# Both halves of the values product in one stretch, instead of one in each half-step behind its job

## What is computed

```python
xn = layernorm(x)
# attention, which norms xn once more with its own gain and bias
q, k, v = (z @ W + b).reshape(B, S, 16, 8)          # z: the second norm
p = (pe @ Wp).reshape(S, 16, 8)
content = einsum('bihd,bjhd->bhij', q + u_bias, k)
pos = relative_shift(einsum('bihd,jhd->bhij', q + v_bias, p))
attn = softmax((content + pos) * 8 ** -0.5)
head = einsum('bhij,bjhd->bihd', attn, v)           # the values product
x = x + head @ Wo + bo + mlp(xn)                    # mlp: 256 -> 512 -> 512 -> 128, relu
```

## Time and profile before

| | |
|---|---|
| median of three runs | 1458.08 us |
| lowest and highest | 1455.66, 1462.42 us |
| profiled execution, first to last instruction | 1453.5 us |
| granted TensorE clock, mean | 0.997 |
| busy TensorE, VectorE, ScalarE, GpSimd | 1441.7, 1357.5, 1226.6, 754.8 us |
| DMA | 550.41 MB, mean 379 GB/s |

### The profile page before, as it was taken

One profiled execution on the slowest core, in us unless ns is written; L12 is line 12 of the kernel. 1 busy time (PEld: TensorE's weight loads), 2 busy tenths in 40 slices (PEclk: granted clock), 3 DMA queues, 4 the chain that ended last, 5 costly groups with the idle time before them and its releaser, 6 DMA issues.

```text
span 1453.5 us, 41653 instructions
## 1 busy us (share of the span) xinstructions
PE 1441.7 (99%) x16170; PEld 977.4 (67%) x16170; DVE 1357.5 (93%) x3489; ACT 1226.6 (84%) x1365; POOL 754.8 (52%) x753
## 2 busy tenths in 40 slices
PE   8999999999999999999999999999999999999999
PEld 4566666666676666766666676666766666666666
DVE  6899999999999999999999999999999999999996
ACT  5688888888888898888888888888888888888874
POOL 5575555555655565454655555566554645543410
PEclk9999999999999999999999999999999999999999
DMA  5999999999999999999999999999999999999992
GB/s 197 385 399 394 383 404 386 389 391 379 409 377 399 394 386 397 377 399 383 397 398 373 408 376 397 397 377 407 382 391 392 384 398 380 394 380 389 396 397 108
DMA packets 80867, 550.41 MB, mean 379 GB/s; under 512 B 9376, under 2 KB 10528, under 8 KB 15136
## 3 DMA queue, kind: packets, MB, share of 16 engines
q1 hardware_dynamic: 43376, 278.61, 49.5%
q10 hardware_dynamic: 37296, 269.15, 47.9%
HBM read 274.57 MB, written 273.15 MB: 377 GB/s over the span
## 4 chain that ended last, share of the span: by engine, by line
PE 95%; DMA 2%; ACT 1%; DVE 1%; issue 0%; SPq 0%; ACTq 0%
PE ps_pt L853 35%; PE ps_av L867 19%; PE ps_pos L829 14%; PE ps_job L756 12%; PE ps_job L720 4%; PE ps_job L710 3%; PE ps_job L735 2%; PE ps_con L841 1%; PE ps_job L731 1%; DMA shift<-pos_sb 1%; ACT pt_sb L514 1%; PE ps_job L743 1%; PE ps_job L726 1%; DMA sc_sb<-shift 1%; DMA heads<-in_pe_t 0%
## 5 line engine op out<-in xcount | busy, mean ns | idle before, releaser
L673 DVE CUSTOM_DVE_ANT_0 sc_sb<-ps_con,sc_sb 128x512 f32<-128x512 f32 x1024 | 661.9, 682 | 65.0 <-PE ps_con L841 61.5
L500 ACT COPY pos_sb<-ps_pos 128x1024 f32<-128x1024 f32 x510 | 518.0, 1016 | 180.4 <-PE ps_pos L829 169.4
L681 DVE TENSOR_SCALAR sc_sb<-sc_sb,nmax 128x512 f32<-128x512 f32 x1024 | 629.2, 646 | 0.1
L853 PE MATMUL ps_pt<-c_sb,sc_sb 128*128 128x128 f32 x4048 | 553.5, 280 | 2.5 <-ACT pt_sb L514 1.5
L514 ACT ACTIVATE pt_sb<-ps_pt 128x1024 f32<-128x1024 f32 x506 | 519.1, 1026 | 20.1 <-PE ps_pt L853 18.8
L853 PEld LDWEIGHTS ps_pt<-c_sb,sc_sb 128*128 128x128 f32 x4048 | 433.9, 141 | 127.1 <-issue 93.2
L867 PE MATMUL ps_av<-pt_sb,v_sb 128*9 128x128 f32 x8192 | 319.9, 274 | 0.1
L867 PEld LDWEIGHTS ps_av<-pt_sb,v_sb 128*9 128x9 f32 x8192 | 172.8, 90 | 184.4 <-issue 182.2
L841 PE MATMUL ps_con<-k_stack,q_stack 26*128 26x512 f32 x1024 | 267.5, 496 | 1.8 <-DVE nmax L673 1.5
L396 POOL CAST h<-act_sb 128x512 fp32r<-128x512 f32 x128 | 78.1, 610 | 360.7 <-ACT act_sb L473 357.4
L829 PE MATMUL ps_pos<-p_stack,q_stack 26*128 26x512 f32 x1024 | 259.6, 496 | 1.2 <-ACT pos_sb L500 0.9
(11 more groups left out here) (116 smaller groups left out, 1015.8 us busy)
## 6 DMA issues: line engine op xcount, KB each, us to landing
shift<-pos_sb SPq DMA_DIRECT2D x256, 1026.0 KB, 9.3
sc_sb<-shift ACTq DMA_DIRECT2D x256, 1024.0 KB, 9.8
x_sb<-in_x SPq DMA_DIRECT2D x16, 256.0 KB, 11.8
out<-x_sb SPq DMA_DIRECT2D x15, 256.0 KB, 10.5
c_sb<-in_consts ACTq DMA_DIRECT2D x1, 288.0 KB, 6.8
sc_sb<-in_wp SPq DMA_DIRECT2D x1, 256.0 KB, 5.8
sc_sb<-in_stack_w ACTq DMA_DIRECT2D x1, 256.0 KB, 5.5
heads<-in_pe_t SPq DMA_DIRECT2D x1, 256.0 KB, 6.9
```

Source lines behind the costliest of these rows:

```text
L500: act.copy(to, ps_pos[:, :, :]).then_inc(s_pe, 1)
L673: dve.tensor_tensor_reduce(sc_sb[:, m % N_SC, t, :], ps_con[:, k, :], sc_sb[:, m % N_SC, t, :], -SCALE, 3.4e38, ALU.add, ALU.min, nmax[:, ...
L681: dve.tensor_scalar(sc_sb[:, m % N_SC, t, :], sc_sb[:, m % N_SC, t, :], nmax[:, m % N_SC, t:t + 1], None, ALU.subtract).then_inc(s_sub, 1)
L853: last = pe.transpose(pt_banks(k)[:, j % 2, t * P:(t + 1) * P], sc_sb[:, u % N_SC, t, j * P:(j + 1) * P], id_sb)
```

## The change

Up to block 500 the values are no longer issued one block to a half, behind the job. In a half whose transposes are those of a unit's first half (k even; these halves are odd), TensorE issues both value blocks of the unit before, k - 2 and k - 1, between the scores and the transposes. In a half with k odd it issues none. `SINGLE` is 2 * 256 - 11 = 501: from the transposes of block 501 on, which stand in half 518, the values stand where they did, and the last units are unchanged. The waits inside `values` and `turn` are the same. `valued` is also what places VectorE's copy of `ps_av`, in the half after the one that does the fourth unit's last block; that half stays the same.

```diff
+        SINGLE = 2 * UNITS - 11
...
         def valued(h):
 
-            return [k - 1 for k in turned(h) if k] + [2 * UNITS - 1] * (h == TURN_AT[-1] + 1)
+            pairs = [v for k in turned(h) if 0 < k < SINGLE and k % 2 == 0 for v in (k - 2, k - 1)]
+            return pairs + [k - 1 for k in turned(h) if k >= SINGLE] + [2 * UNITS - 1] * (h == TURN_AT[-1] + 1)
...
                 turns, products = turned(half), valued(half)
+                if products and products[0] < SINGLE - 1:
+                    for k in products:
+                        values(*divmod(k, 2))
+                    products = []
                 for k in turns[:1]:
                     turn(*divmod(k, 2))
                 for j in parts(half):
```

## The result

Four runs of the changed kernel gave 1483.14 to 1486.87 us, a median of 1484.56, against 1456.87 for the kernel before on the same chip. The ratio is 1.0185, 95% interval 1.0159 to 1.0212. Lines of the changed kernel stand three further down: the transposes are line 856, the values 870, the exponential 517, reduce and subtraction 676 and 684.

A forecast was written before the change was run, and what follows sets the result against it. TensorE, busy 99%, sets the pace, VectorE and ScalarE close behind. Per batch -1.76 + 2.43 + 0.4 + 0.3 = about +1.35, over 15.5 batches +21: span 1474.5, plus 4.6 around it, 1479 us; range 1461 to 1492.

The forecast's parts named there:

- Handover saved: Two value blocks back to back on TensorE save one handover per unit: 0.11 each, 1.76 per batch.
- (c): Scores to values in the long half costs 0.33, not 0.44: 3.5 saved per batch against 3.1 of waits, 1452; chance 0.09.
- (d): TensorE handovers at the mean of three kinds: 0.17 saved per unit, 2.7 per batch against 3.1, 1465; chance 0.06.
- Wait for the exponential: Short half's transposes, without values before them, wait for the long half's exponential: 2.43 per batch.
- the 2.27 from load to load: Least distance the exponential allows between transposes of adjacent halves with no job between: 2.27 us.
- its sign of being wrong: Forecast is wrong if, among other signs, the short half's transposes start under 2.2 after the long half's.
- ScalarE's chain: Exponential, evacuation, score copy and next exponential delay the long half's second value block: about 0.4 per batch.
- VectorE's rhythm: Uneven halves make VectorE's reduces late for the second contents product: 1.15 per batch, net 0.3 after today's waits.
- The walk: Stepping VectorE through a batch with today's intervals: contents late 0.45 by half 3, 0.42 at half 17; 1.15 per batch.
- Ends: Halves with no job at both ends wait 0.8 instead of 0.25: 2 more, less 2 where waits coincide.
- Rival (a): The exponential's wait swallows ScalarE's and VectorE's knock-on waits: 0.67 x 15.5 = 10, plus 2 at the ends, 1470; chance 0.20.
- Rival (b): VectorE stays late after short halves, reduces on the path in a third of units: another 0.7 per batch, 1490; chance 0.10.

The follow-up runs named there:

- e7: Changed kernel with the exponential of each unit's first half split by bank and GpSimd's split instructions cut to 64 columns; 1436.04 us (0.9854).
- e1: Kernel before with GpSimd's two split instructions cut to 64 of 512 columns from the third batch on; 1448.37 us (0.9957).
- e2: Changed kernel with GpSimd's two split instructions cut to 64 of 512 columns from the third batch on; 1457.24 us (1.0017).
- e9: Kernel before with values paired only in two units of 16, long halves 21 and 31 of 32; ratio 1.0015.
- e3: Kernel before with its single value block per half moved between scores and transposes, one half later, and the ps_av copy behind VectorE's reduces; 1482.34 us (1.0196).

## Why the prediction was right, and which term was off

The forecast was 1479 us, the result 1484.56, inside the range; the side and the two mechanisms hold. By the prediction's own steps:

- **Handover saved**, -1.76 per batch: -1.78 in e7 against e1, and 0.11 in halves 22 and 23 by themselves. Scores to values 0.44, job to scores as job to values. Right, and with it rivals (c) and (d) fall.
- **Wait for the exponential**, +2.43: 1.87 in e2. The places are right (halves 4, 8, 12, 20, 24, 30 with 0.3 each; 10, 16, 28 with 0.05), the size 0.56 too large. The step that was off is the 2.27 from load to load, read from one pair of halves; there the bracket of the second row names VectorE's subtraction as what came last, and not the exponential. In the kernel after it is 2.20 (743.55 to 745.75), since 0.05 and not 0.12 passes behind the exponential. That is the very edge of what the prediction had called its sign of being wrong. The code says that these are waits for `s_exp`, and the split exponential took them away. The total that the profile puts down to the exponential rose from 10 to 83.4 us, not to some 45.
- **ScalarE's chain**, +0.4: 0.1 to 0.2, a term too small to matter.
- **VectorE's rhythm**, net +0.3: about 1.5, the difference between 1.85 and 0.31. This is the term that was mis-sized, by a factor of five. The walk took "the intervals of today" for VectorE, and these don't stay: a subtraction's time depends on whether GpSimd is at work, and the change moves the jobs that GpSimd follows. I had counted only how late VectorE would start, not that its work would grow by 43 us. The walk's gross figure was 1.15, with 0.45 in half 3 and 0.42 in half 17; in the long halves contents are late by 1.82, with 0.19 in half 3 and 0.67 in half 17. The netting against today's 0.8 was too much as well: late contents are only 0.37 of that in the trace before, and the cut on GpSimd took 0.48 off a batch.
- **Ends**, +2 less 2: 28.7 of the span's 31.5 are 15.5 batches of 1.85, so 2.8 are left.

The trace before already held what was missed. The 3.43 that the prediction takes from the earlier trace rows isn't the distance of two scores, as it says, but that of VectorE's first reduces in two halves, and inside it lies a subtraction that GpSimd had made long:

```profile
709.10 1.28 DVE L681 TENSOR_SCALAR sc_sb<-sc_sb,nmax 128x512 f32<-128x512 f32 x1
```
```profile
708.83 1.27 POOL L387 TENSOR_TENSOR k_stack<-act_sb,k_stack 128x512 fp32r<-128x512 f32 x1
```

Part of the hit is luck. Exponential and ScalarE were 0.8 too high, VectorE 1.2 too low, so the batch came to +1.85 and not +1.35. And the 4.6 us that were added for what lies around the span were 1.8 to 1.9 in every run measured since: the forecast missed the time by 5.6 us, but the spans, 1481.3 to 1485.0, lie 7 to 10.5 above its 1474.5.

Rival (a), that the knock-on waits are swallowed, is close to what the runs with the cut show, 9 us, and wrong for the full kernel. Rival (b), with +2.05 per batch, 1490 us and late contents in a third of the units, is as near to the result as the forecast, and nearer in its batch and its reason: contents are late in the long halves of 6 of the 16 units. It had the right engine, but VectorE isn't late for good; its late starts come back in the same halves of every batch, and what makes it late is its own longer subtractions.

TensorE's busy time did not fall or stay, as the prediction had it, but rose by 12 us. The same 1024 contents products show 295.6 us busy instead of 267.5, at 0.494 and 0.496 us for one; a second product that comes late overlaps the first less. Busy time isn't work.

What stays open is how much of VectorE's 1.5 is overlap with GpSimd in the strict sense and how much is a fuller VectorE meeting an unevenly spaced TensorE. The cut takes both away at once, as it also frees 0.15 us per subtraction. A run with GpSimd's work whole and VectorE's cut otherwise wasn't made.

## What to carry to other kernels

A block that is moved on the bounding engine is also a cover that is moved: list for each wait what stands between its two ends before and after, and its price follows from start-to-start distances. Where two engines slow each other down, durations read from the old trace are no constants; a change that only shifts jobs in time can add work on an engine it doesn't touch. And in a schedule with just 0.8 us of waits in 87.6, look for the price of a local saving some halves further on: the pair in halves 20 and 21 saved 0.13 where it stood and cost 0.37 in half 24.

## What the runs showed that I had not expected

A subtraction of 128x512 in SBUF takes 0.47 to 0.49 us alone, and beside GpSimd anything from that to 1.6 (the kernel after, median 0.89); the reduces, which read PSUM too, take 0.65 to 0.69 whatever GpSimd does. The Trainium skill, "SBUF — State Buffer", section "SBUF: two separate sides", says that the port pair shared by VectorE and GpSimd is an exclusive lock held for a whole instruction, and not a split of bandwidth. The rows agree: in the kernel after the first of the two subtractions of 770.05 lasts 1.25 us and ends 0.3 behind GpSimd's instruction of 769.74 to 771.01, and the pair takes 2.08. In e9 the one of 779.54 ends 0.3 behind GpSimd's of 779.32 to 780.60.

Starting each job 0.55 us later within its half, with the values ahead of it and VectorE's copy of `ps_av` behind its reduces, cost 2.1 us per batch (e3, 89.77 against 87.63), more than the 1.85 of the paired version.
